# Counting edges: the second one-hot laid out with its steps innermost, and read by TensorE with a stride

## The chip, the cores and the metric

The kernel runs on one core of one Trainium2 chip. The metric is the device time of the whole program in microseconds (us), the median of three runs; lower is better.

## The reference

The reference is a stack of four graph layers (a GraphConv with batch norm, a SAGE layer pair, an attention layer and two relational layers) on 3125 nodes with 128 features and 103125 directed edges. All four take the same edge list, sorted by destination. The first two need, for every node, the sum of its neighbours' feature rows:

```
edge_index = jnp.stack([src, dst])
h = jnp.maximum(_layernorm(x, axis=-1), 0.0)
aggr = jax.ops.segment_sum(h[src], dst, num_segments=x.shape[0])      # layer 0
h = aggr @ W_rel + b_rel + x @ W_root                                 # then batch norm, relu, + x
agg = jax.ops.segment_sum(h[edge_src], edge_dst, num_segments=N) * inv_deg   # layer 1, twice
```

## The kernel before

The kernel does those sums as dense products with a matrix of edge counts, adj, which it builds first and keeps in DRAM. This stage, the edge counting, is the one that the change touches; it runs from about 62 us to 484 us of the profiled execution. Everything after it (the dense products of L794, the attention rounds, the relational layers with their gathers) is the same in both kernels.

**What is counted.** The edges lie in 806 tiles of 128, sorted by destination. A step is one tile of edges against one block of four destination nodes. There are 1596 steps, in 84 epochs of 19 (`EPOCHS`, `STEPS_OF`). For one step, an edge with source node s and destination d becomes two one-hot rows: one of 128 for the low seven bits of s (`hot_lo`), and one of 100 (`CELLS`) for its cell, which joins the high bits of s (25 values) with the place of d in the block (4 values) (`hot_cell`). TensorE multiplies the two, with the 128 edges as the contraction: the result, 128 x 100, holds the edge counts of this step, and adds up in PSUM at the place of its block.

**The three engines of an epoch.** VectorE makes the one-hots of an epoch in two instructions (`compare_epochs`): L677 compares `iota_lo` (the numbers 0 to 127, each written 19 times in a row) with the epoch's low bits, and L679 compares `iota_cell` (the numbers 1 to 100, once) with the epoch's cell numbers. There are two buffers of each one-hot; the comparison of epoch e waits until the matmuls of epoch e - 2 are done (`estep_n`). TensorE (`count_edges`) loads the epoch's 20 places from `steprow` into registers (L694), clears four PSUM banks with matmuls of zeros (L702, which waits for the eviction of epoch e - 2), waits for the one-hots of the epoch (`ehot_n`), issues 19 matmuls with one register operation ahead of each for the place (L706), then adds the overlap with the epoch before from SBUF (L711, which waits for the eviction of epoch e - 1), and closes the four banks (L715). ScalarE (`move_out`) evicts the half of PSUM into a window in SBUF (L737). Four epochs fill one window, and SP stores it to adj in DRAM (L759, 3850 KB). Between epochs 16 and 41 VectorE also takes the moments of one tile of x per epoch (L487).

**The layouts.** The low one-hot has the step innermost: its columns for one step lie 19 elements of 2 bytes, that is 38 bytes, apart. TensorE loads it as the weights of the step. The cell one-hot has the cell innermost, so the 100 columns of one step lie side by side. TensorE reads it as the moving operand.

**Before the stage.** `iota_ci` (int32, 1 to 100) is copied to `iota_cell` in L293 on ScalarE, and `iota_lo` written in L294. L362 writes `los`, L404 writes `cells`. `bs` (`step_block`) holds the block of every step, 1596 numbers, until L402.

Of the kernel before, what the change touches and what calls it, by code (L numbers as in the profile page):

```python
# [7 lines left out]
F16 = mybir.dt.float16  # L8
B16 = mybir.dt.bfloat16
ALU = mybir.AluOpType  # L10
ACT = mybir.ActivationFunctionType
# [3 lines left out]
P = 128  # L15
# [30 lines left out]
CELLS = HI * WD  # L46
KT = 7
STEPS_OF = 19
# [3 lines left out]
STEPS = EPOCHS * STEPS_OF  # L52
# [59 lines left out]
def build(nc, a, out):  # L112
    with ExitStack() as ctx:
# [6 lines left out]
        V = Lane(nc.vector, sem("s_dve"))  # L120
        A = Lane(nc.scalar, sem("s_act"))
# [20 lines left out]
        B1T = trio[:, NP:2 * NP]  # L142
# [62 lines left out]
        dense = ExitStack()  # L205

        def tmp(stack, name, shape, dt=F32):
            return stack.enter_context(nc.sbuf_tensor(name, shape, dt))
# [3 lines left out]
        los = tmp(dense, "edge_lo", [P, EPOCHS, STEPS_OF], F16)  # L212
        cells = tmp(dense, "edge_cell", [P, EPOCHS, STEPS_OF], F16)
        iota_lo = tmp(dense, "iota_lo", [P, P, STEPS_OF], F16)
        iota_cell = tmp(dense, "iota_cell", [P, CELLS], F16)
        steprow = tmp(dense, "steprow", [1, EPOCHS, 32], I32)
        dstf = invdeg[:, 4 * P:(4 + KT) * P].rearrange("p (k e) -> p k e", e=P)
        relf = invdeg[:, (4 + KT) * P:(4 + 2 * KT) * P].bitcast(F16)[:, 0:KT * P].rearrange("p (k e) -> p k e", e=P)
# [4 lines left out]
        early = ExitStack()  # L223
# [12 lines left out]
        iota_ci = tmp(early, "iota_ci", [P, CELLS], I32)  # L236
# [1 line left out]
        pid = tmp(early, "pid", [P, KT])  # L238
        first_d = tmp(early, "block_first", [P, KT])
        starts = tmp(early, "block_starts", [P, KT])  # L240
        bs = tmp(early, "step_block", [P, STEPS])
        rels = iota_si[:, :].bitcast(F32)
        inside = lower[:, 0:2 * STEPS].bitcast(F32)
        b0 = tmp(early, "epoch_block", [1, EPOCHS])
# [40 lines left out]
        cio = G.did(G.after().iota(iota_ci[:, :], pattern=[[1, CELLS]], base=1, channel_multiplier=0))  # L285
# [4 lines left out]
        G.did(G.after().iota(pieceidx[:, :], pattern=[[P, PT]], base=0, channel_multiplier=1))  # L290
        ios = A.did(A.after(sio).activation(iota_s[:, :], iota_si[:, :], ACT.Copy))
        iof = A.did(A.after(io).activation(iota[:, :], iota_i[:, :], ACT.Copy))
        A.did(A.after(cio).activation(iota_cell[:, :], iota_ci[:, :], ACT.Copy))  # L293
        A.did(A.after().activation(iota_lo[:, :, :], iota[:, :].unsqueeze(2).to_broadcast([P, P, STEPS_OF]), ACT.Copy))  # L294

        V.did(V.after(pio).tensor_copy(pid[:, :], pid_i[:, :]))
# [3 lines left out]
        for g in range(KT):  # L300
            m = V.did(nc.vector.tensor_scalar(lower[:, g * ET:(g + 1) * ET], dlast[:, :], first_d[:, g:g + 1], 0.0,
                                              ALU.is_lt, ALU.add, accum_out=starts[:, g:g + 1]))
# [3 lines left out]
        for g in range(KT):  # L306
            m = V.did(nc.vector.tensor_scalar(past[:, g, :], iota_s[:, :], starts[:, g:g + 1], None, ALU.is_ge))
# [22 lines left out]
        for k in range(KT):  # L330
            m = V.did(nc.vector.tensor_scalar(at_tile[:, k, :], ts[:, :], pid[:, k:k + 1], None, ALU.is_equal))
# [22 lines left out]
        for b, terms in ((4, (0,)), (0, (1,))):  # L354
            for j in range(4):
                for k in range(KT):
                    m = nc.tensor.matmul(pb[b + j][:, 0:QUARTER], digits[:, terms[0], k, :],
                                         at_tile[:, k, j * QUARTER:(j + 1) * QUARTER],
                                         start=(k == 0), stop=(k == KT - 1))
            looked = T.did(m)  # L360
            if b == 4:
                lod = A.did(A.after(looked).activation(los[:, :, :].rearrange("p e k -> p (e k)")  # L362
                                                       .rearrange("p (j c) -> p j c", c=QUARTER),
                                                       bank[:, 4:8, 0:QUARTER], ACT.Copy))
        T.need(lod)
        for j in range(4):
            for k in range(KT):
                for q in (2, 3):
                    m = nc.tensor.matmul(pb[4 + j][:, 0:QUARTER], digits[:, q, k, :],
                                         at_tile[:, k, j * QUARTER:(j + 1) * QUARTER],  # L370
                                         start=(k == 0 and q == 2), stop=(k == KT - 1 and q == 3))
# [272 lines left out]
        def turn_bank(j, src, folded, add):  # L644
            T.need(folded[j])
            tiles = tiles_of_bank(j)
            for i, t in enumerate(tiles):
# [6 lines left out]
        filled = [tmp(build, "adj_window", [P, SPANNED * CELLS]), arena[:, 0:SPANNED * CELLS]]  # L654
        LO, CELL = P * STEPS_OF // 2, STEPS_OF * CELLS // 2
        hot_lo = [t[:, 0:LO].bitcast(F16).rearrange("p (l k) -> p l k", k=STEPS_OF) for t in (B1T, HT)]
        hot_cell = [B1T[:, LO + j * CELL:LO + (j + 1) * CELL].bitcast(F16).rearrange("p (k c) -> p k c", c=CELLS)
                    for j in (0, 1)]
        G.need(V.now(), T.now(), A.now())
        wiped = [G.did(nc.gpsimd.memset(filled[j][:, SLOTS * CELLS * (1 - j):], 0.0)) for j in (0, 1)]  # L660
# [5 lines left out]
        first_norm = {}  # L666

        def compare_epochs():
            V.after()
            for e in range(EPOCHS):  # L670
                if e == 1:
                    V.need(s_seg.now())
                if e == MOMENTS_FROM:
                    V.need(s_x.now())
                if e > 1:
                    nc.vector.wait_ge(estep_n, e - 1)
                nc.vector.tensor_tensor(hot_lo[e % 2][:, :, :], iota_lo[:, :, :],  # L677
                                        los[:, e, :].unsqueeze(1).to_broadcast([P, P, STEPS_OF]), ALU.is_equal)
                nc.vector.tensor_tensor(hot_cell[e % 2][:, :, :],  # L679
                                        iota_cell[:, :].unsqueeze(1).to_broadcast([P, STEPS_OF, CELLS]),  # L680
                                        cells[:, e, :].unsqueeze(2).to_broadcast([P, STEPS_OF, CELLS]),
                                        ALU.is_equal).then_inc(ehot_n, 1)
                if MOMENTS_FROM <= e < MOMENTS_FROM + NT:
                    tile_moments(X, [e - MOMENTS_FROM])
                if e == VARIANCE_AT:
                    first_norm["variance"] = rows_variance(0, NT)
                if e == SHIFT_AT:
                    first_norm["shift"] = rows_shift(0, NT, (root_n, 1))

        def count_edges():  # L690
            T.need(stepped, A.now())
            for e in range(EPOCHS):
                half = sums[:, (e % 2) * 2048:(e % 2 + 1) * 2048]
                place = nc.values_load_multi_w_load_instructions(  # L694
                    steprow[0:1, e, 0:SLOTS], engines=(ENG.PE,), min_val=0, max_val=(SPANNED - 1) * CELLS,
                    skip_runtime_bounds_check_because="made on the chip from counts")[1]
                place = [nc.s_assert_within(v, 0, 2048 - CELLS, skip_runtime_bounds_check_because="made on the chip")
                         for v in place[:STEPS_OF]] + [place[STEPS_OF]]
                if e > 1:
                    nc.tensor.wait_ge(eout_n, e - 1)  # L700
                for j in range(4):
                    nc.tensor.matmul(half[:, j * 512:j * 512 + SLOTS // 4 * CELLS], zeros[:, 0:P],  # L702
                                     zeros[:, 0:SLOTS // 4 * CELLS], start=True, stop=False)
                nc.tensor.wait_ge(ehot_n, e + 1)
                for k in range(STEPS_OF):
                    m = nc.tensor.matmul(half[:, bass.ds(place[k], CELLS)], hot_lo[e % 2][:, :, k], hot_cell[e % 2][:, k, :],  # L706
                                         start=False, stop=False)
                m.then_inc(estep_n, 1)
                if e:
                    nc.tensor.wait_ge(eout_n, e)  # L710
                    nc.tensor.matmul(half[:, 0:CELLS], ident[:, :],  # L711
                                     filled[(e - 1) // GROUP % 2][:, bass.ds(place[STEPS_OF], CELLS)],
                                     start=False, stop=False)
                for j in range(4):
                    m = nc.tensor.matmul(half[:, j * 512:j * 512 + 1], zeros[:, 0:P], zeros[:, 0:1], start=False, stop=True)  # L715
                m.then_inc(ebuilt_n, 1)
# [60 lines left out]
        dense = ExitStack()  # L777
# [123 lines left out]
        for c in range(NCH):  # L901
# [4 lines left out]
            m = T.did(nc.tensor.matmul(pb[b][:, 0:CH], Wt["L0_root"][:, :], HT[:, s], start=False, stop=True))  # L906
# [7 lines left out]
        m = V.did(V.after().tensor_scalar(var, var, EPS, None, ALU.add))  # L914
        m = A.did(A.after(m).activation(bn["sd"][:, :], var, ACT.Sqrt))
# [4 lines left out]
        m = V.did(V.after().tensor_tensor(bn["shift"][:, :], bn["shift"][:, :], bcol["L0_beta"][:, :], ALU.add))  # L920
# [3 lines left out]
        for b, tiles in groups():  # L924
            m = A.did(nc.scalar.activation(cols_of(HT, tiles), cols_of(B1T, tiles), ACT.Relu, bias=bn["shift"][:, 0:1],
                                           scale=bn["scale"][:, 0:1]))
            T.need(m, last_evac[b])
            for j, t in enumerate(tiles):
                m = T.did(nc.tensor.transpose(pb[b][:, j * P:(j + 1) * P], HT[:, t * P:(t + 1) * P], ident[:, :]))
# [43 lines left out]
        for g in range(0, NT + 4, 4):  # L973
            tiles = list(range(g, min(g + 4, NT)))
            if tiles:
                b, m = products(tiles, "L1_n0", "L1_s0")
# [91 lines left out]
        m = V.did(V.after().tensor_scalar(pairnode[:, :], pairnode[:, :], 1.0, None, ALU.add))  # L1068
# [361 lines left out]
        for g in range(0, PAIRS, 4):  # L1430
# [3 lines left out]
            for j in js:  # L1434
                m = nc.tensor.transpose(pb[b][:, (j - g) * P:(j - g + 1) * P], pairs[:, j * P:(j + 1) * P], ident[:, :])
            m = T.did(m)
# [15 lines left out]
        m = V.now()  # L1452
# [230 lines left out]
```

## Time and profile before

| | |
|---|---|
| median of three runs | 4267.49 us (4274.33, 4267.49, 4263.15) |
| span of the profiled execution | 4266.3 us |
| time of the profiled execution beside the span | none given; its span lies 1.2 us under the median |
| TensorE matmul busy in the span | 3043.3 us (71%) |
| VectorE busy | 2017.8 us (47%) |
| GpSimd busy | 2364.9 us (55%) |
| edge counting, first to last DVE compare | 62.4 to 475.6 us |

The span is the time from the first instruction to the last on the core. PE is TensorE's matmuls, PEld its weight loads, PEldq and PEq its sequencer; DVE is VectorE, ACT ScalarE, POOL GpSimd, SP SyncE. A busy share over the whole span mixes stages; the prediction reads the edge counting alone. "issue" is idle time for which the profile shows no releaser. PEclk is the granted clock of TensorE, 1.00 for 2.4 GHz and 0.50 for 1.2 GHz.

### The profile page before, as it was taken

How to read it: one execution, taken by the hardware profiler on the slowest of the kernel's cores; microseconds unless marked ns; L12 is line 12 of the kernel's file. 1: busy time of each engine (PE TensorE's matmuls, PEld its weight loads, DVE VectorE, ACT ScalarE, POOL GpSimd, SP SyncE). 2: the span in 40 equal slices, each digit the busy share in tenths (PEclk: the TensorE clock that was granted, in tenths of full speed). 3: DMA queues.
4: the chain of work that ended last, by engine and by line, in shares of the span. 5: the costliest groups of instructions: out<-in, count | busy, mean ns of one | idle time of the engine just before them, and what ended most of it. 6: DMA issues, size and time to landing. Idle time of an engine off the chain costs nothing.

```text
span 4266.3 us, 42581 instructions
## 1 busy us (share of the span) xinstructions
PE 3043.3 (71%) x12281; PEld 2000.6 (47%) x12281; DVE 2017.8 (47%) x4124; ACT 705.0 (17%) x1923; POOL 2364.9 (55%) x2466
## 2 busy tenths in 40 slices
PE   5666798996888888888376666666667666666666
PEld 3555454554666666565243333333344333433334
DVE  7777685467988888898631111111112111111112
ACT  2334201002444444343320000000001000000000
POOL 3000000004777777776237777777775777777776
PEclk8778898998999999899675555555557555555555
DMA  3544754463444444443041111111123111111112
GB/s 125 214 191 194 302 215 190 200 263 97 119 115 114 118 110 118 110 118 97 3 149 53 53 53 53 53 53 52 53 70 142 53 53 53 52 53 53 52 53 63
DMA packets 236740, 456.14 MB, mean 107 GB/s; under 512 B 64036, under 2 KB 183570, under 8 KB 231392
## 3 DMA queue, kind: packets, MB, share of 16 engines
q1 hardware_dynamic: 158728, 291.44, 18.8%
q0 software_dynamic: 77792, 161.98, 13.9%
q8 instruction: 113, 1.85, 0.2%
q14 instruction: 107, 0.88, 0.1%
HBM read 336.68 MB, written 116.51 MB: 106 GB/s over the span
## 4 chain that ended last, share of the span: by engine, by line
POOL 37%; PE 26%; issue 17%; DMA 15%; DVE 4%; ACT 2%; SPq 0%; ACTq 0%; DVEq 0%; POOLq 0%
POOL edge_buffers L574 21%; POOL round_buffers L1124 16%; DMA edge_buffers<-rel_table,relidx 13%; PE sums L794 9%; PE sums L602 4%; PE sums L706 3%; PE sums L702 3%; PE sums L1582 2%; PE sums L711 1%; ACT adj_window L737 0%; DMA adj<-adj_window 0%; ACT chunk_and_window L737 0%; DMA adj_chunk<-adj 0%; PE sums L1246 0%; DVE tile_moments L487 0%
## 5 line engine op out<-in xcount | busy, mean ns | idle before, releaser
L574 POOL DMA_INDIRECT edge_buffers<-rel_table,relidx x1612 | 1534.2, 952 | 586.0 <-PE sums L602 268.8
L602 PE MATMUL sums<-edge_buffers 128*128 128x128 f32 x3224 | 1254.7, 495 | 750.2 <-DMA edge_buffers<-rel_table,relidx 746.4
L602 PEld LDWEIGHTS sums<-edge_buffers 128*128 128x128 f32 x3224 | 802.1, 310 | 1206.0 <-issue 1205.1
L585 DVE TENSOR_SCALAR edge_buffers<-iota,rel 128x128 f32<-128x128 f32 x1612 | 335.2, 296 | 1644.4 <-PE sums L602 1644.4
L1124 POOL DMA_INDIRECT round_buffers<-xs_t,srcs x806 | 765.5, 950 | 570.9 <-DMA xd_t<-round_buffers 325.5
L631 ACT ACTIVATE trio<-sums,c_L_b 128x256 f32<-128x256 f32 (+1 forms) x16 | 8.0, 500 | 2020.4 <-PE sums L606 2020.4
L944 POOL IOTA trio<- 128x806 int32 x1 | 0.8, 805 | 603.8 <-ACT H L517 603.8
L1168 PE MATMUL sums<-round_buffers,ident 128*128 128x408 f32 x620 | 278.6, 533 | 27.6 <-DMA round_buffers<-xs_t,srcs 24.1
L1171 PEld LDWEIGHTS sums<-round_buffers 128*128 128x128 f32 x1612 | 243.5, 198 | 76.1 <-issue 65.6
L1268 ACT ACTIVATE trio<-sums 128x128 f32 x806 | 223.7, 278 | 279.7 <-PE sums L1246 196.7
L1171 PE MATMUL sums<-round_buffers 128*128 128x136 f32 x1612 | 244.8, 285 | 0.0
L1246 PE MATMUL sums<-round_buffers 128*128 128x128 f32 x1612 | 241.7, 300 | 3.7 <-DVE round_buffers L1329 2.0
L794 PE MATMUL sums<-chunk_and_window,H 128*128 128x448 f32 x600 | 232.4, 548 | 7.7 <-issue 6.4
L1246 PEld LDWEIGHTS sums<-round_buffers 128*128 128x128 f32 x1612 | 217.3, 210 | 17.4 <-issue 14.5
L702 PE MATMUL sums<-zeros 128*128 128x500 f16 x336 | 110.4, 463 | 134.8 <-issue 131.7
L1320 DVE TENSOR_TENSOR positive<-positive,sums 128x384 f32<-128x384 f32 x310 | 153.1, 494 | 71.7 <-ACT positive L1258 71.4
L679 DVE TENSOR_TENSOR trio<-iota_cell,edge_cell 128x1900 f16<-128x1900 f16 x84 | 179.0, 2130 | 0.0
L677 DVE TENSOR_TENSOR trio<-iota_lo,edge_lo 128x2432 f16<-128x2432 f16 x84 | 125.2, 1491 | 112.4 <-PE sums L706 110.0
L794 PE MATMUL sums<-adj_chunk,H 128*128 128x448 f32 x450 | 172.4, 543 | 2.3 <-DMA adj_chunk<-adj 2.3
L794 PEld LDWEIGHTS sums<-chunk_and_window,H 128*128 128x128 f32 x600 | 115.5, 194 | 120.4 <-issue 118.6
L1309 DVE TENSOR_SCALAR round_buffers<-sums,pair_column 128x416 f32<-128x416 f32 x248 | 159.9, 645 | 11.5 <-PE sums L1186 10.3
L706 PEld LDWEIGHTS sums<-trio 128*128 128x128 f16 x1596 | 149.2, 151 | 28.7 <-issue 17.6
(289 smaller groups left out, 3000.0 us busy)
## 6 DMA issues: line engine op xcount, KB each, us to landing
chunk_and_window<-adj SPq DMA_DIRECT2D x10, 5600.0 KB, 15.8
round_buffers<-xd_t SPq DMA_DIRECT2D x806, 68.0 KB
adj_chunk<-adj SPq DMA_DIRECT2D x9, 5600.0 KB, 16.5
adj<-adj_window SPq DMA_DIRECT2D x11, 3850.0 KB, 11.5
adj<-chunk_and_window SPq DMA_DIRECT2D x10, 3850.0 KB, 11.3
edge_buffers<-rel_table,relidx POOLq DMA_INDIRECT x1612, 2.5
rel_table<-table_stages SPq DMA_DIRECT2D x50, 512.0 KB, 2.6
round_buffers<-xs_t,srcs POOLq DMA_INDIRECT x806, 2.5
```

The lines of the kernel that those rows point to most:

```text
L574: nc.gpsimd.indirect_dma_start(slot(t), None, table[:, :], bass.IndirectOffsetOnAxis(ap=index[:, t:t + 1], axis=0)).then_inc(slot_sem(t), 16)
L585: made = nc.vector.tensor_scalar(round_hots(i)[:, k, :], iota[:, :], rel[:, t:t + 1], None, ALU.is_equal)
L602: nc.tensor.matmul(sums[:, bass.ds(place[k], P)], slot(t), round_hots(i)[:, k, :], start=False, stop=False).then_inc(summed_n, 1)
L679: nc.vector.tensor_tensor(hot_cell[e % 2][:, :, :], iota_cell[:, :].unsqueeze(1).to_broadcast([P, STEPS_OF, CELLS]), cells[:, e, :].unsque ...
L702: nc.tensor.matmul(half[:, j * 512:j * 512 + SLOTS // 4 * CELLS], zeros[:, 0:P], zeros[:, 0:SLOTS // 4 * CELLS], start=True, stop=False)
L706: m = nc.tensor.matmul(half[:, bass.ds(place[k], CELLS)], hot_lo[e % 2][:, :, k], hot_cell[e % 2][:, k, :], start=False, stop=False)
L794: m = nc.tensor.matmul(ps.rearrange("p (b w) -> p b w", w=WD), tables[:, hi, :], held[b][:, :, hi, :], start=(hi == 0), stop=(hi == HI - 1))
L1124: nc.gpsimd.indirect_dma_start(rows[r % RING][:, k * RW:(k + 1) * RW], None, xs_t[:, :], bass.IndirectOffsetOnAxis(ap=srcs[:, t:t + 1], ax ...
L1168: nc.tensor.matmul(pb[2 + q % 2][:, 0:(hi - lo) * RW], ident[:, :], rows[r % RING][:, lo * RW:hi * RW], start=True, stop=False)
L1171: m = nc.tensor.matmul(pb[2 + q % 2][:, (k - lo) * RW:(k - lo + 1) * RW], hotT[r % 2][:, k * P:(k + 1) * P], win[r % 2][:, k * RW:(k + 1) ...
L1246: m = nc.tensor.matmul(pb[6 + q % 2][:, (k - lo) * P:(k - lo + 1) * P], msg[:, k * P:(k + 1) * P], hot[r % 2][:, k * P:(k + 1) * P], start ...
L1268: nc.scalar.activation(pairs[:, bass.ds(at[k], P)], pb[6 + q % 2][:, (k - lo) * P:(k - lo + 1) * P], ACT.Copy).then_inc(out_n, 1)
```

## The change

The numbers 1 to 100 are now written 19 times each (`iota_cell` is 128 x 100 x 19), the cell one-hot has the step innermost as the low one has, and L679 becomes an instruction whose three operands all run along 19 neighbouring elements. TensorE's moving operand `hot_cell[e % 2][:, :, k]` then has its 100 elements 38 bytes apart. To write the larger table ScalarE loses the copy of 100 elements ahead of `iota_lo` and gets one of 1900 elements behind L362; VectorE waits for it once, ahead of the first epoch. `bs` moves into a free part of `B1T`, which makes room in SBUF; nothing else changes its place.

```
-        iota_cell = tmp(dense, "iota_cell", [P, CELLS], F16)
+        iota_cell = tmp(dense, "iota_cell", [P, CELLS, STEPS_OF], F16)
-        bs = tmp(early, "step_block", [P, STEPS])
+        bs = B1T[:, 0:STEPS]
-        A.did(A.after(cio).activation(iota_cell[:, :], iota_ci[:, :], ACT.Copy))
+        A.need(cio)
                                                        bank[:, 4:8, 0:QUARTER], ACT.Copy))
+        cells_numbered = A.did(nc.scalar.activation(iota_cell[:, :, :],
+                                                    iota_ci[:, :].unsqueeze(2).to_broadcast([P, CELLS, STEPS_OF]), ACT.Copy))
-        hot_cell = [B1T[:, LO + j * CELL:LO + (j + 1) * CELL].bitcast(F16).rearrange("p (k c) -> p k c", c=CELLS)
+        hot_cell = [B1T[:, LO + j * CELL:LO + (j + 1) * CELL].bitcast(F16).rearrange("p (c k) -> p c k", k=STEPS_OF)
-            V.after()
+            V.after(cells_numbered)
-                nc.vector.tensor_tensor(hot_cell[e % 2][:, :, :],
-                                        iota_cell[:, :].unsqueeze(1).to_broadcast([P, STEPS_OF, CELLS]),
-                                        cells[:, e, :].unsqueeze(2).to_broadcast([P, STEPS_OF, CELLS]),
+                nc.vector.tensor_tensor(hot_cell[e % 2][:, :, :], iota_cell[:, :, :],
+                                        cells[:, e, :].unsqueeze(1).to_broadcast([P, CELLS, STEPS_OF]),
                                         ALU.is_equal).then_inc(ehot_n, 1)
-                    m = nc.tensor.matmul(half[:, bass.ds(place[k], CELLS)], hot_lo[e % 2][:, :, k], hot_cell[e % 2][:, k, :],
+                    m = nc.tensor.matmul(half[:, bass.ds(place[k], CELLS)], hot_lo[e % 2][:, :, k], hot_cell[e % 2][:, :, k],
```

On ScalarE's queue the start of the program reads, before:

```order
 L291 ACTIVATE iota_s<-chunk_and_window 128x1596
 L292 ACTIVATE iota<-iota_i 128x128
-L293 ACTIVATE iota_cell<-iota_ci 128x100
 L294 ACTIVATE iota_lo<-iota 128x2432
 L320 ACTIVATE digits<-hi_i 128x896
 L321 ACTIVATE digits<-hi_i 128x896
 L362 ACTIVATE edge_lo<-sums 128x1596
```

The row marked with a minus is gone from there in the changed kernel. The same queue of the changed kernel, from the evacuation of the low bits (`edge_lo`) to the transposed weights (`w_L_...`) and the loads of the stage, with its own line numbers:

```order
6 L362 ACTIVATE edge_lo<-sums 128x1596
7 L365 ACTIVATE iota_cell<-iota_ci 128x1900
8 L414 ACTIVATE w_L_s<-sums 128x128
9 L414 ACTIVATE w_L_n<-sums 128x128
10 L414 ACTIVATE w_L_s<-sums 128x128
11 L414 ACTIVATE w_L_n<-sums 128x128
12 L722 TENSOR_LOAD epochrow
```

The copy stands between L362 and the weights, where nothing stood before, and has grown from 100 to 1900 elements. On VectorE and TensorE no instruction changes its place.

## Rows read from the trace of the kernel before

**Rows 1.** The page, group 5: busy, mean ns of one, idle before and releaser

```profile
L679 DVE TENSOR_TENSOR trio<-iota_cell,edge_cell 128x1900 f16<-128x1900 f16 x84 | 179.0, 2130 | 0.0
L677 DVE TENSOR_TENSOR trio<-iota_lo,edge_lo 128x2432 f16<-128x2432 f16 x84 | 125.2, 1491 | 112.4 <-PE sums L706 110.0
```

**Rows 2.** The timeline of TensorE's matmuls, one window of four epochs

```profile
223.86 1.46 PE L702 MATMUL sums<-zeros 128*128 128x500 f16 x4 [0.90 <-issue]
230.76 1.53 PE L702 MATMUL sums<-zeros 128*128 128x500 f16 x4 [3.27 <-issue]
232.09 1.79 PE L706 MATMUL sums<-trio 128*128 128x100 f16 x19
233.68 0.71 PE L711 MATMUL sums<-adj_window,ident 128*128 x2
234.19 0.29 PE L715 MATMUL sums<-zeros 128*128 128x1 f16 x4
235.82 1.00 PE L702 MATMUL sums<-zeros 128*128 128x500 f16 x4 [1.35 <-issue]
236.66 1.85 PE L706 MATMUL sums<-trio 128*128 128x100 f16 x19
239.81 1.00 PE L702 MATMUL sums<-zeros 128*128 128x500 f16 x4 [0.90 <-issue]
240.65 1.91 PE L706 MATMUL sums<-trio 128*128 128x100 f16 x19
242.43 0.46 PE L711 MATMUL sums<-adj_window,ident 128*128 x2
242.73 0.24 PE L715 MATMUL sums<-zeros 128*128 128x1 f16 x4
243.87 1.00 PE L702 MATMUL sums<-zeros 128*128 128x500 f16 x4 [0.90 <-issue]
```

**Rows 3.** The line of the places' load: duration ns min/median/max, first and last start

```profile
L694 PEldq TENSOR_LOAD <-steprow x84: 1356/1383/4776, 64.5 to 477.5; - x84
```

**Rows 4.** The line of the 19 matmuls, 235.8 to 238.35 us only

```profile
L706 PEldq FUSED_REGOPS  x19: 37/37/42, 235.8 to 238.2; - x19
L706 PEld LDWEIGHTS sums<-trio x19: 136/138/159, 236.5 to 238.3; 128*128 128x128 f16 x19
```

**Rows 5.** The same line, 232.0 to 233.65 us (a stretch at half clock)

```profile
L706 PE MATMUL sums<-trio x19: 286/286/289, 232.1 to 233.6; 128*128 128x100 f16 x19
```

**Rows 6.** The line of the clearing matmuls, 235.7 to 236.4 us

```profile
L702 PEld LDWEIGHTS sums<-zeros x4: 96/96/96, 235.8 to 236.2; 128*128 128x128 f16 x4
```

**Rows 7.** The timeline of VectorE in the same window

```profile
226.94 1.49 DVE L677 TENSOR_TENSOR trio<-iota_lo,edge_lo 128x2432 f16<-128x2432 f16 x1 [0.60 <-PE sums L706]
228.35 2.13 DVE L679 TENSOR_TENSOR trio<-iota_cell,edge_cell 128x1900 f16<-128x1900 f16 x1
230.39 0.29 DVE L487 BATCH_NORM_STATS2 tile_moments<-X 128x6 f32<-128x128 f32 x1
235.33 2.13 DVE L679 TENSOR_TENSOR trio<-iota_cell,edge_cell 128x1900 f16<-128x1900 f16 x1
```

**Rows 8.** The timeline of SP's queue, 220 to 250 us

```profile
225.07 0.33 SPq L759 DMA_DIRECT2D adj<-chunk_and_window  x1
```

**Rows 9.** The timeline of ScalarE: the start, and one eviction

```profile
4.44 0.29 ACT L293 ACTIVATE iota_cell<-iota_ci 128x100 f16<-128x100 int32 x1
4.76 2.23 ACT L294 ACTIVATE iota_lo<-iota 128x2432 f16<-128x2432 f32 x1
18.89 0.95 ACT L320 ACTIVATE digits<-hi_i 128x896 bf16<-128x896 int32 x1 [11.90 <-DVE hi_i L319]
63.62 0.28 ACT L412 ACTIVATE w_L_s<-sums 128x128 f32<-128x128 f32 x1 [22.44 <-PE sums L409]
234.59 1.84 ACT L737 ACTIVATE adj_window<-sums 128x2000 f32 x1 [5.10 <-PE sums L715]
```

**Rows 10.** The chain that ended last, in the dense products: start, us, what

```profile
541.43 18.79 PE sums L794 x50
```

**Rows 11.** The page, group 6: DMA issues, KB each, us to landing

```profile
adj<-adj_window SPq DMA_DIRECT2D x11, 3850.0 KB, 11.5
```

## The prediction

> **What bounds the kernel now.** The change touches the edge counting alone, so I read that stage and not the shares of the whole span. First the page's groups: per epoch VectorE spends 1.491 us on the low one-hot and 2.130 us on the cell one-hot, and the only wait in front of them is 110 us in all on TensorE's matmuls of L706 [rows 1]. So VectorE waits for TensorE in this stage. Then TensorE's timeline over one window of four epochs [rows 2]: L702 starts at 223.86, 230.76, 235.82, 239.81 and 243.87, which makes epochs of 6.90, 5.06, 3.99 and 4.06 us, 20.01 us a window; 21 windows are 420 us. Ahead of each L702 TensorE is idle for 0.90 to 3.27 us with no releaser named. The line of the places' load names it: this register load takes 1.36 us at least and 4.78 us at most [rows 3]. The long ones fall right behind the store of a window, which SP issues at 225.07 [rows 8] and which lands 11.5 us later [rows 11]: I take them for loads that queue behind that store. Last, the pace inside an epoch: TensorE's sequencer issues the 19 register operations of L706 from 235.8 to 238.2, 2.4 / 18 = 0.13 us apart (with the first one's wait for the clearing matmuls; in the middle 0.12) [rows 4]. An epoch of the short kind is therefore 1.36 us of load and some 2.65 us of issue, 4.0 us: the **sequencer of TensorE** bounds it, not the array and not VectorE.
>
> How far VectorE is from the path: the one-hots of the comparison at 226.94 are done at 228.35 + 2.13 = 230.48, and the matmuls that read them start at 236.66 [rows 2, 7]; those done at 235.33 + 2.13 = 237.46 are read at 240.65. That is 6.2 and 3.2 us of slack.
>
> **VectorE's part.** L677 shows what the new form costs: 2432 elements in rows of 19 in 1491 ns. L679 with 1900 elements in the same form takes, in proportion, 1165 ns, and with a fixed part of some 150 ns set aside 1200 ns. I take 1200: 930 ns less per epoch, 84 x 0.93 = 78 us less busy time. None of it is on the path, since the slack above is larger than 0.93 us already; VectorE will wait longer for L706 instead. Its gain is 0. If the form did not speed up at all (bound from above), the result would be the same 0.
>
> **ScalarE's part.** The removed copy took 0.29 us, and 11.90 us of idle time stand behind L294 before L320 [rows 9]: 0. The new copy of 1900 elements lies between the 2.23 us of L294's 2432 elements and nothing, so about 1.8 us. It starts when L362 ends, near 41 us, and ScalarE is idle for 22.44 us until 63.62 [rows 9]; the first comparison comes at 62.4. TensorE's queue waits for L362 by its own mark, not for the new copy. 0, and if the cover were gone at most 1.8 us, once. Moving `bs` costs nothing: the same instructions on another address.
>
> **TensorE's part, the term that decides.** Each of the 1596 matmuls now reads its 100 moving columns 38 bytes apart. No matmul of the trace reads a moving operand so, therefore bounds. Contiguous, at half clock the 19 matmuls start from 232.1 to 233.6, 1.5 / 18 = 83 ns apart, which is 100 columns at 1.2 GHz [rows 5]; at full clock this is 42 ns. Free reading is the lower bound (nothing added). From above: L794 reads its moving operand in 112 runs of four elements of 4 bytes, 400 bytes apart, and takes 18.79 / 50 = 376 ns [rows 10], so a jump costs 3.36 ns at most; 100 jumps are 336 ns. Between them stands the nearest row, the weights of L706, which have this very stride: their load takes 138 ns, the contiguous weights of L702 take 96 ns [rows 4, 6]. The stride costs 42 ns on 128 columns. Spread over all 128 that is 0.33 ns a column, and a matmul would take 42 + 33 = 75 ns. If the load brings its columns in four at a time, 32 one behind the other, it is 1.3 ns a column, and a matmul takes 42 + 131 = 173 ns. I take the second, **170 ns**: a weight load that delivered one column at a time at the moving operand's full rate would already take 128 columns x 0.42 = 53 ns of its 96, and the rows of L715, four loads and matmuls in 0.24 us with their latency [rows 2], leave no room for 53 ns each.
>
> The page "Advanced Engine Details and Errata" of the Trainium skill, section SBUF Cachelines, says that SBUF has lines of 16 bytes, and that a reader needs two hits on a line to hide the memory's latency. A stride of 38 bytes hits each line once, so the rule speaks against this change; no run here shows its size for a moving operand. Read as "half the rate" it would give 83 ns a matmul at full clock, which the sequencer's 120 ns hide.
>
> From 170 ns the epoch follows. At full clock the array needs 0.84 us from L702's start to L706's (239.81 to 240.65), 19 x 0.17 = 3.23, then 0.30 for L711 and 0.10 for L715 (242.43 to 242.73, and four short ones) [rows 2]: 4.47 us. At half clock L702 takes about 1.5 and L711 with L715 0.6: 5.3 us. The load of the places runs beside the array's backlog, so an epoch takes the larger of sequencer and array:
> - 42 epochs of the short kind: 4.47 in place of 4.03, 42 x 0.44 = 18.5 us.
> - 21 second epochs at 5.06: hidden at full clock, 0.24 at half clock; taken as half of them, 3 us.
> - 21 first epochs of 6.90: the array is hidden, but matmuls that end later make the eviction later (1.84 us, [rows 9]), L711 waits for it, and the load queued behind L711 starts later: about 0.25, 5 us.
>
> Sum 26.5 us, all on the path, against a span of 4266.3: 4293 us. Added to the median, 1.2 us higher, **4294 us**. Behind the wait of L711 stand on TensorE's queue only L715 and the next load, counted above.
>
> **Rivals.**
> - A. No change. The strided read takes up to 115 ns a matmul (the 75 ns reading above, or half rate), and the sequencer's pace covers it: 4267 us. For it: 3.2 us of slack, and 45 to 78 ns of cover per matmul. Against: the array would have to read this stride at a seventh to a third of the jump price that L794 allows, which no row shows.
> - B. Much slower. Weights and moving operand now both jump through SBUF in the same instants and hinder each other: 240 ns a matmul, an array epoch of 0.84 + 4.56 + 0.40 = 5.8 us, so 42 x 1.77 + 21 x 0.9 + some 5 = 98 us: 4366 us. At the bound of 336 ns every epoch is array-bound at 7.6 us, 21 x (30.5 - 20.0) = 220 us: 4487 us. Nothing in the trace rules it out.
> - C. Faster. The long loads of the places are slowed not by the store alone but also by VectorE's traffic, of which 0.93 us per epoch goes. The loads beyond 1.36 us cost (6.90 - 4.0) + (5.06 - 4.0) = 4.0 us a window, 84 us in all; it needs a matmul of at most 115 ns, and if a quarter of the excess were the comparison's it gives 21 us: 4246 us. Against: the comparisons run in all four epochs, the excess stands only in the two behind the store. It decides from a tenth of the excess on.
>
> That L679 keeps its 2.13 us is part of A where the read is free: same time.
>
> **Chances.** The forecast, a matmul of 120 to 200 ns, 0.45; A 0.37; B 0.13; C 0.05. This kernel's measurement tells about 0.3% (13 us) from no change. Of the forecast's cases about 0.04 add less than 13 us (140 ns or below). So faster 0.05, same 0.40, slower 0.55. The likeliest case's own range is 4277 to 4325; the range that should hold eight in ten must take in A and the near half of B: 4262 to 4370.
>
> **What will show it.** In the profile of the changed kernel: L681 (the cell comparison) at about 1200 ns; a longer wait of L679 for the matmuls, by some 80 us and more; the new copy under 2 us near 41 us with idle time behind it. The step that decides is the spacing of the matmuls of L707 in a full-clock epoch: 0.17 us and an epoch of 4.5 us prove the forecast, 0.12 and 4.0 prove A, 0.24 and 5.8 prove B. The load of the places should still take 1.36 us at least; shorter long ones would speak for C. The prediction is wrong if the stage from the first comparison to the last eviction does not grow by 13 to 60 us, or if the time moves elsewhere.

## The result: slower by 1.9%, three times the forecast loss

The changed kernel takes 4348.91 us (median) against 4265.33 us before in the same session: ratio 1.0192, 95% interval 1.0175 to 1.0208, 84 us more by the medians. The forecast was 4294 us, 27 us more. One of the changed kernel's four executions took 11346.93 us, far from the others and unexplained; the ratio leaves it out, and the median of the other three is 4343.97 us. The direction and the strided read as its source came as forecast. The size did not, although 4348.91 us lies inside the stated range.

The page of the changed kernel begins so (span, then the same groups as in [rows 1]; L679 and L681 are the two comparisons there, L707 the 19 matmuls, L703 the clears):

```profile
span 4352.5 us, 42582 instructions
L707 PE MATMUL sums<-trio 128*128 128x100 f16 x1596 | 306.9, 362 | 0.0
L679 DVE TENSOR_TENSOR trio<-iota_lo,edge_lo 128x2432 f16<-128x2432 f16 x84 | 125.4, 1493 | 271.5 <-PE sums L707 268.2
L703 PE MATMUL sums<-zeros 128*128 128x500 f16 x336 | 149.2, 597 | 33.4 <-issue 31.7
```

Its line for the cell comparison, with duration min/median/max:

```profile
L681 DVE TENSOR_TENSOR trio<-iota_cell,edge_cell x84: 1190/1194/1200, 63.9 to 557.9; 128x1900 f16<-128x1900 f16 x84
```

VectorE got what it was to get, 1194 ns in place of 2130. It waits 268.2 us for the matmuls where it waited 110.0 [rows 1]. TensorE's timeline of one window, which answers to [rows 2]:

```profile
275.94 1.83 PE L703 MATMUL sums<-zeros 128*128 128x500 f16 x4
277.56 3.65 PE L707 MATMUL sums<-trio 128*128 128x100 f16 x19
281.03 0.60 PE L712 MATMUL sums<-adj_window,ident 128*128 x2
281.42 0.29 PE L716 MATMUL sums<-zeros 128*128 128x1 f16 x4
281.58 1.83 PE L703 MATMUL sums<-zeros 128*128 128x500 f16 x4
283.20 3.67 PE L707 MATMUL sums<-trio 128*128 128x100 f16 x19
286.68 0.59 PE L712 MATMUL sums<-adj_window,ident 128*128 x2
288.55 1.82 PE L703 MATMUL sums<-zeros 128*128 128x500 f16 x4 [1.19 <-issue]
294.46 1.82 PE L703 MATMUL sums<-zeros 128*128 128x500 f16 x4
```

Two things have changed. From L707's start to L712's, 19 matmuls, it is 286.68 - 283.20 = 3.48 us: **183 ns a matmul**. And most of the 0.90 to 3.27 us waits ahead of the clears are gone. TensorE is idle for 33.4 us in all ahead of L703; ahead of the same clears before it was 134.8 us:

```profile
L702 PE MATMUL sums<-zeros 128*128 128x500 f16 x336 | 110.4, 463 | 134.8 <-issue 131.7
```

The epochs of 5.64 us (275.94 to 281.58) hold no idle time, so the array bounds them. The clears start some 0.42 us apart at half clock, and 1.62 us go from L703's start to L707's, where the full-clock epoch of before had 0.84.

The stage as a whole, by the view of stretches, of before and of the changed kernel (busy of PE, PEld, DVE, ACT, POOL; then the granted clock):

```profile
68.14:484.20 416.06, 283.57 (x2434) 221.71 (x2432) 298.71 (x199) 165.37 (x111) 7.71 (x2) 0.81 0.47 198
```

```profile
68.14:570.30 502.16, 471.20 (x2434) 319.83 (x2434) 222.46 (x199) 165.44 (x111) 7.82 (x2) 0.56 0.40 168
```

The stage is 86.1 us longer and the span 86.2 us: all of the loss is here. What follows takes 4266.3 - 484.2 = 3782.1 us before and 4352.5 - 570.3 = 3782.2 us after. The granted clock of the stage fell from 0.81 to 0.56: 67 of the 83 distances between epochs run at half clock throughout, where it was 14 before. Where the clock is full, the changed kernel's epoch is shorter with the same matmuls:

```profile
162.11 1.00 PE L703 MATMUL sums<-zeros 128*128 128x500 f16 x4
162.95 3.63 PE L707 MATMUL sums<-trio 128*128 128x100 f16 x19
166.40 0.56 PE L712 MATMUL sums<-chunk_and_window,ident 128*128 x2
166.91 1.41 PE L703 MATMUL sums<-zeros 128*128 128x500 f16 x3
```

This epoch takes 166.91 - 162.11 = 4.80 us, with 182 ns a matmul. **The 19 strided matmuls take the same time at either clock; the clears and L712 do not**, and they make the 0.84 us by which the epoch of 5.64 us is longer. (The clock is full up to L712 here, which takes 0.56 us as at half clock.)

### The profile page after: what moved, and what is told of

Read it like the earlier page. It is cut to its first block, busy times and chain, and to the rows that moved or that the text cites. A ratio compares the mean times of both kernels' runs of the same rounds, so it can differ in the third digit from the quotient of the medians.

```text
span 4352.5 us, 42582 instructions
## 1 busy us (share of the span) xinstructions
PE 3225.0 (74%) x12281; PEld 2094.8 (48%) x12281; DVE 1940.1 (45%) x4124; ACT 706.3 (16%) x1923; POOL 2369.7 (54%) x2466
## 4 chain that ended last, share of the span: by engine, by line
PE 34%; DMA 24%; POOL 24%; issue 12%; DVE 5%; ACT 1%; SPq 1%; DVEq 0%; ACTq 0%; POOLq 0%
DMA edge_buffers<-rel_table,relidx 22%; POOL round_buffers L1125 13%; POOL edge_buffers L576 10%; PE sums L795 9%; PE sums L604 7%; PE sums L707 7%; PE sums L703 3%; PE sums L1583 2%; PE sums L1169 1%; PE sums L712 1%; PE sums L1247 1%; PE sums L1172 1%; DVE logits L1324 1%; DVE positive L1321 0%; DMA adj_chunk<-adj 0%
## 5 line engine op out<-in xcount | busy, mean ns | idle before, releaser
L707 PE MATMUL sums<-trio 128*128 128x100 f16 x1596 | 306.9, 362 | 0.0
L707 PEld LDWEIGHTS sums<-trio 128*128 128x128 f16 x1596 | 227.2, 142 | 101.5 <-issue 41.1
L679 DVE TENSOR_TENSOR trio<-iota_lo,edge_lo 128x2432 f16<-128x2432 f16 x84 | 125.4, 1493 | 271.5 <-PE sums L707 268.2
L703 PE MATMUL sums<-zeros 128*128 128x500 f16 x336 | 149.2, 597 | 33.4 <-issue 31.7
```

## The experiments

Stage means from the first comparison to the end of the last eviction: 421.8 us before, 507.8 us in the changed kernel. Runs e5 to e10 were taken on two other chips, on which the whole program is some 850 us longer, the kernel before too (5120 us). In e5's trace the extra time lies behind the edge counting (4629 us against 3782). The kernel before left no trace on those chips, so their stages are set beside the 421.8 us from the first one; that this may be done is borne out by e5, whose stage and the changed kernel's agree to 0.1 us. Differences of whole programs are of the medians.

### e1: the read alone, first try

```
-        hot_cell = [... .rearrange("p (k c) -> p k c", c=CELLS)
+        hot_cell = [... .rearrange("p (c k) -> p k c", k=STEPS_OF)
```

> Only the read is changed: VectorE makes the cell one-hot with the operands of before (100 cells innermost, the cell number repeated), but writes it with the step innermost, so that TensorE's moving columns lie 38 bytes apart as in the changed kernel. Output as the reference's. Theory (TensorE's strided read costs 183 ns a matmul and the clock stays at half): all of the loss is here, 4340 to 4360 us, the matmuls 183 ns apart, epochs of 5.6 us, although the comparison keeps about 2.1 us. Rival (the new comparison or the new copy takes part in the loss, for instance by disturbing TensorE's reads of SBUF): clearly under 4340 us, spacing under 183 ns.

Measured: 4649.26 us, ratio 1.0908 (1.0891 to 1.0924). This was a bad experiment. VectorE now writes each element 38 bytes from the last, and that is what the run shows:

```profile
L679 DVE TENSOR_TENSOR trio<-iota_cell,edge_cell x84: 8381/8408/8437, 62.7 to 864.6; 128x1900 f16<-128x1900 f16 x84
```

8.41 us in place of 2.13 makes VectorE the bound (no idle time before either comparison). It says nothing on the size of the loss, except that the matmuls stand 183 ns apart here too, with a quite different VectorE beside them.

### e5: the read alone, with VectorE as before

```
+        step_of = [f.rearrange("p (c k) -> p c k", k=STEPS_OF) for f in flat_cell]
-  ... hot_cell[e % 2][:, k, :],
+  ... step_of[e % 2][:, :, k],
```

> The read alone, with VectorE exactly as before (both comparisons write as before, 1.49 and 2.13 us); TensorE takes its 100 moving columns 38 bytes apart from the same buffer, so the edge counts are not those of the reference. Theory (the loss is TensorE's strided read and nothing else): 4344 to 4354 us, spacing 183 ns, epochs of 5.6 us, the clock at half nearly throughout. Rival (the new comparison helps or hurts beside it): off by more than 10 us from the changed kernel.

Measured: ratio 1.0181 (1.0156 to 1.0205), 84 us more than before; the stage 507.7 us against the changed kernel's 507.8. The cell comparison kept its 2.13 us. The timeline has the same epoch:

```profile
276.07 1.83 PE L703 MATMUL sums<-zeros 128*128 128x500 f16 x4
277.69 3.65 PE L707 MATMUL sums<-trio 128*128 128x100 f16 x19
281.16 0.60 PE L712 MATMUL sums<-adj_window,ident 128*128 x2
281.70 1.83 PE L703 MATMUL sums<-zeros 128*128 128x500 f16 x4
```

The read makes the whole loss. With 3.62 us of comparisons or 2.69, an epoch takes 5.63 to 5.64 us. The read also brings the clock down: it is the only change against the kernel before, and the granted clock of the stage is 0.55 where it was 0.81.

### e2: the comparison alone

```
-  ... hot_lo[e % 2][:, :, k], hot_cell[e % 2][:, :, k],
+  ... hot_lo[e % 2][:, :, k], flat_cell[e % 2][:, k * CELLS:(k + 1) * CELLS],
```

> Only the comparison is changed: the one-hots are made as in the changed kernel (comparison of 1.19 us), but TensorE reads 100 neighbouring elements as the moving operand, so the edge counts are not those of the reference. Theory (VectorE is off the path): 4262 to 4270 us, no change from before, VectorE waits for the matmuls some 80 us more. Rival (VectorE's time counts in the short epochs, or its traffic lengthens the loads of the places): 4240 to 4255 us, short epochs under 4.0 us or the long loads under 4.3 us.

Measured: 4263.48 us against 4264.02, ratio 1.0002 (0.9993 to 1.0011); stage 421.7 us. Nearly all of the 78 us that VectorE saves becomes wait, 185.2 us for the matmuls in place of 110.0:

```profile
DVE trio L679 <- PE sums L707: 185.2, 82, 5.3
```

So rival C is out, which needed a gain of 8 us or more: neither VectorE's time nor its traffic was in the loads of the places, of which 20 still take 4.3 us or more, as before.

### e3: half of the columns

```
+  half[:, bass.ds(place[k], CELLS // 2)], hot_lo[e % 2][:, :, k], hot_cell[e % 2][:, 0:CELLS // 2, k],
```

> The changed kernel, but every matmul of the counting reads only the first 50 of its 100 strided columns (the other half of the counts is left out). Theory (a price of 1.83 ns per column read, whatever the clock): 92 ns a matmul at most, which the sequencer's 120 ns hide, so the loss is gone: 4262 to 4272 us. Rival (a fixed price for a matmul with a strided operand): spacing stays over 150 ns and the time over 4310 us.

Measured: 4267.88 us, ratio 1.0011 (1.0002 to 1.0021), the matmuls 95 to 96 ns apart. Half of the columns cost half of the time, so the price goes by the column. This run also separates the clock from the loss; its stage:

```profile
68.14:484.00 415.86, 342.65 (x2408) 251.49 (x2407) 221.97 (x199) 162.85 (x110) 7.22 (x2) 0.50 0.46 194
```

The granted clock was half throughout, and the whole stage took 426.9 us, 5 us more than before. Here, where the array has room to spare, half clock costs at most these 5 us; in the changed kernel, where the array bounds the epochs, it costs 0.84 us an epoch.

### e4: a table of strides in one run

Each window of four epochs reads its operands in another way:

```
+  READS = ((1, 19, 100), (2, 19, 100), ..., (19, 1, 100), (1, 1, 100), ..., (19, 19, 50), (19, 19, 25))
+  return (flat_lo[e % 2][:, k:k + ws * (P - 1) + 1:ws], flat_cell[e % 2][:, ko:ko + s * (n - 1) + 1:s], n)
```

> A table in one run: the 21 windows of four epochs read the operands of the counting matmuls with 21 combinations of the moving stride (1 to 19 elements of 2 bytes), the weights' stride (19, 4 or 1) and the number of columns (100, 75, 50, 25); the edge counts are not those of the reference. Theory (a moving column costs 1.83 ns once each lies on a line of its own, less below, and the weights have no part): about 183 ns at strides of 8 elements and more, falling below that, the same with contiguous weights, 137 ns with 75 columns, the sequencer's 120 ns or the backlog's 60 ns with 50 and 25. Rival (weights and moving operand hinder each other): with contiguous weights at moving stride 19 the spacing falls clearly, towards 100 ns.

Measured in one execution (4308.72 us): from the starts of the matmuls in the trace, the median distance in the window's epochs in ns (s: moving stride in elements of 2 bytes, w: stride of the weights, n: columns). Strides 1 and 2 are given where the array has a backlog at full clock; elsewhere the sequencer or the clock sets their distance.

```
w 19, n 100:  s 1: about 60   s 2: 63   s 3: 77   s 4: 97   s 5: 119   s 6: 140   s 7: 162   s 8: 184
              s 9: 188   s 10: 186   s 12: 182   s 16: 186   s 18: 184   s 19: 183
other:        s 19 w 1: 180   s 8 w 1: 179   s 4 w 4: 94   s 19 n 75: 139   s 19 n 50: 95   s 19 n 25: 60
```

Four rows of its timeline at stride 5, then four at stride 8, then two with contiguous weights (L714 are the clears, L719 the matmuls, L724 what follows):

```profile
143.73 2.43 PE L719 MATMUL sums<-trio 128*128 128x100 f16 x19
145.98 0.38 PE L724 MATMUL sums<-chunk_and_window,ident 128*128 x2
151.45 2.45 PE L719 MATMUL sums<-trio 128*128 128x100 f16 x19
153.72 0.66 PE L724 MATMUL sums<-adj_window,ident 128*128 x2
...
225.25 1.83 PE L714 MATMUL sums<-zeros 128*128 128x500 f16 x4
226.87 3.68 PE L719 MATMUL sums<-trio 128*128 128x100 f16 x19
230.37 0.60 PE L724 MATMUL sums<-chunk_and_window,ident 128*128 x2
230.91 1.83 PE L714 MATMUL sums<-zeros 128*128 128x500 f16 x4
...
395.49 3.61 PE L719 MATMUL sums<-trio 128*128 128x100 f16 x19
398.92 0.59 PE L724 MATMUL sums<-adj_window,ident 128*128 x2
```

(145.98 - 143.73) / 19 = 118 ns, (230.37 - 226.87) / 19 = 184 ns, (398.92 - 395.49) / 19 = 181 ns. From stride 3 to 8 the distance grows by 20 to 22 ns per element of stride, and then it stays between 180 and 188 ns. A stride of 8 elements is 16 bytes. So the price is about **1.84 ns for each piece of 16 bytes that the read newly touches**: at stride 8 and above each column touches one, at stride 4 two columns share one (50 x 1.84 = 92, measured 97). This is a fit to the table, good to 2 ns from stride 6 to 8 and 4 to 8 ns too low from 3 to 5. Contiguous weights take off 3 to 5 ns: the two operands hardly hinder each other, and rival B's mechanism is out.

The page "Advanced Engine Details and Errata" of the Trainium skill, section SBUF Cachelines, has the 16 bytes right, by this table. Its "at least two hits on a cacheline" is not enough for this 2-byte moving operand: stride 4 has two hits and takes 97 ns, where stride 1 shows about 60 and single distances down to 44 ns.

### e6: does more dense work bring the clock back?

```
-                for j in range(4):
+                for j in range(8):      # the second four add zeros
```

> The changed kernel, with the four clearing matmuls of each epoch issued twice (the second four add zeros). It adds 0.84 us of dense array work per epoch at full clock, 1.67 us at half. Theory (the half clock comes from the strided reads, which leave the array waiting for its operand, and 19 x 0.183 us of them per epoch keep it down whatever stands beside them): epochs of 5.63 + 1.67 = 7.3 us, some 4455 us. Rival (more dense work brings the full clock back): 4.80 + 0.84 = 5.6 us an epoch, 4350 us, and the granted clock of the stage well over 0.56.

Measured: 5286.92 us, ratio to before 1.0337; stage 584.8 us, 77 us over the changed kernel's. The view of stretches:

```profile
100.00:480.00 380.00, 357.71 (x1822) 227.64 (x1821) 149.58 (x143) 104.57 (x62) 0.00 (x0) 0.76 0.34 144
```

Neither expectation holds alone. The granted clock rose from 0.56 to 0.76, with nothing but the four added clears an epoch: so the strided matmuls do not hold the clock at half whatever stands beside them. But every window still has epochs at half clock in part or throughout, and the time lies between the two forecasts. Some epochs run at full clock from end to end:

```profile
250.65 1.85 PE L703 MATMUL sums<-zeros 128*128 128x500 f16 x8
252.33 3.63 PE L707 MATMUL sums<-trio 128*128 128x100 f16 x19
256.11 1.85 PE L703 MATMUL sums<-zeros 128*128 128x500 f16 x8
```

This one takes 256.11 - 250.65 = 5.46 us; without the second four clears (0.84 us) it would be 4.62 us, an estimate of the changed kernel's epoch at full clock. That the strided read brings the clock down is shown by e5, and that dense work beside it brings part of it back by e6; what it is in the strided matmuls that does it stays open.

### e7: a layout that TensorE reads cheaply

```
+ iota_cell = tmp(dense, "iota_cell", [P, CELLS, 4], F16)
+ hot_cell = [t[:, LO:LO + SLOTS * CELLS // 2].bitcast(F16).rearrange("p (g c k) -> p g c k", k=4, c=CELLS) for t in (B1T, HT)]
+ ... hot_cell[e % 2][:, k // 4, :, k % 4],
```

> The cell one-hot in groups of four steps, the step of the group innermost: VectorE's operands run along 4 neighbouring elements, TensorE's moving columns lie 8 bytes apart; the output is the reference's. Theory (a matmul costs 1.84 ns for each line of 16 bytes that it newly reads, two columns to a line here): about 97 ns, under the sequencer's 120 ns, 4260 to 4270 us, no change from before, with the comparison at 1.2 to 1.3 us. Rival (short rows cost VectorE its gain, or a spacing of 97 ns at half clock still delays the evictions): over 4275 us.

Measured: ratio 1.0018 (1.0002 to 1.0035); stage 422.6 us, before's 421.8. The comparison takes 1.46 us, not 1.2 to 1.3, and the matmuls stand 97 ns apart:

```profile
240.03 1.00 PE L706 MATMUL sums<-zeros 128*128 128x500 f16 x4 [0.85 <-issue]
240.87 1.98 PE L710 MATMUL sums<-trio 128*128 128x100 f16 x19
242.72 0.46 PE L715 MATMUL sums<-adj_window,ident 128*128 x2
244.16 1.00 PE L706 MATMUL sums<-zeros 128*128 128x500 f16 x4 [0.90 <-issue]
```

An epoch takes 244.16 - 240.03 = 4.13 us with 0.90 us of idle time, as in [rows 2]. The loss is gone and VectorE keeps 0.67 us per epoch, which nothing needs. The granted clock is 0.81 over the stage as before, although the matmuls stand as far apart as in e3, where it was 0.50: the distance alone does not decide the clock.

### e8 to e10: is it the sequencer that paces the kernel before?

e8 is the kernel before with three loads of places a window (20, 32 and 28 numbers) in place of four of 20:

```
+                if e % GROUP == 1 and e > 1:
+                    place = ahead
+                elif e % GROUP == 0 and e:
+                    got = load_places(e * SLOTS + 12, 28)
+                    place, ahead = [*ahead, *got[:8]], got[8:]
+                elif e % GROUP == 3 and e < EPOCHS - 1:
+                    got = load_places(e * SLOTS, 32)
+                    place, ahead = got[:SLOTS], got[SLOTS:]
```

> The kernel before, with the places of a window loaded by three register loads in place of four, and none in the epoch right behind the store's start (20, 32 and 28 numbers, each used one epoch later at the latest); comparisons, matmuls and layouts as before. Theory (the sequencer of TensorE with these loads paces the epochs): a window loses 1.4 us at least and 3.3 us where the slow load goes with it, 21 x 1.4 to 3.3 = 29 to 69 us, so 4195 to 4236 us, limited by VectorE's 3.6 to 3.9 us per epoch. Rival (the array, VectorE or the eviction sets the pace, and the loads are slow because something else is late): within 10 us of before.

Measured: stage 406.2 us against 421.8, 15.6 us less; the whole program 5110.59 against 5119.94 us, ratio 0.9985 (0.9971 to 1.0000), an interval that reaches no change. This is less than the 29 to 69 us expected. The line of the loads (duration ns min/median/max), and the clears of two epochs in the timeline:

```profile
L693 PEldq TENSOR_LOAD <-steprow x64: 1360/2130/4910, 64.8 to 462.2; - x64
```

```profile
239.48 1.00 PE L716 MATMUL sums<-zeros 128*128 128x500 f16 x4 [0.85 <-issue]
242.27 1.00 PE L716 MATMUL sums<-zeros 128*128 128x500 f16 x4
```

The epoch without a load takes 242.27 - 239.48 = 2.8 us (median 2.98 in the 21 windows), where a short epoch with its load took 4.0, so the load was on the path. But 32 numbers take 2.13 us and 28 take 1.88 where 20 take 1.36, in proportion to their count; and the first load behind the start of the window's store still takes some 4.4 us, only one epoch later. Of what was saved, this leaves 0.75 us a window.

e9 puts e8's loads and e7's layout together.

> The three register loads a window of e8, with the one-hot in groups of four steps of e7; the output is the reference's. Theory (the loads and the issue of TensorE's sequencer pace the stage, VectorE stays off the path even in the shorter windows): the stage as in e8, 406 us, some 4249 us where the kernel before takes 4265. Rival (in e8 VectorE's 3.6 to 3.9 us held back the epoch without a load): clearly shorter than e8, 395 us and 4238 us or less.

Measured: 5105.00 against 5121.69 us, ratio 0.9974 (0.9960 to 0.9989); stage 408.8 us, e8's 406.2. VectorE's 0.67 us bring nothing even here. This is the only version whose interval lies below 1, by 0.1 to 0.4%; by the stage alone e8 is as good or 2.6 us better.

e10 puts e8's loads into the changed kernel.

> The changed kernel with the three register loads a window of e8. Theory (with the strided read the array bounds the epochs, 5.6 us, and the loads run beside it, except the slow one): only the place of the slow load moves, windows of 23.9 us in place of 24.1, 4340 to 4349 us. Rival (the sequencer still paces the changed kernel, its loads late because the queue is full): as large a gain as in e8 or larger, 4333 us or less.

Measured: ratio to before 1.0166 (1.0138 to 1.0193); stage 501.9 us, 5.9 us under the changed kernel's. The epoch without a load, 2.8 us in e8, takes 284.78 - 279.13 = 5.65 us here at half clock (median 5.43):

```profile
279.13 1.83 PE L717 MATMUL sums<-zeros 128*128 128x500 f16 x4
280.75 3.67 PE L721 MATMUL sums<-trio 128*128 128x100 f16 x19
```

So the sequencer paces the kernel before, and the array the changed one.

## Why the prediction was wrong

- **VectorE's gain of 930 ns an epoch is worth 0**: right. 936 ns were measured, and e2 made no difference (1.0002).
- **ScalarE's copy is hidden**: right. It took 1.78 us at 41.18 us, with 20.77 us of idle time behind it.
- **What bounds the stage before**: right. The sequencer with its loads, shown by e8 and e10. That the long loads queue behind the store is borne out by e8, where the load that now meets the store's start is the long one.
- **170 ns a matmul**: near, 183 ns, but partly by luck. The prediction drew 131 ns from the weights of the same stride and added them to the 42 ns of 100 columns at full clock. With the 83 ns of half clock the same sum gives 214 ns, and 183 were measured at half clock too. Nor do the weights pay the moving operand's price: 128 x 1.84 would be 236 ns, and their load takes 140. So "four columns at a time" is not shown; it only gave a number near the right one. Rival A (75 or 83 ns) and rival B (240 ns, for a reason that e4 excludes) were wrong. In rival B's sum 21 x 0.9 should be 21 x 0.74 by its own 5.8 and 5.06 us, 3 us less; nothing rests on it.
- **"At full clock the array needs ... 4.47 us. At half clock ... 5.3 us", and then 42 short epochs at 4.47**: this step failed. The prediction took the clock of before over into the changed kernel. With 183 ns the two figures are 4.80 and 5.64 us, both seen in the trace; but nearly all epochs ran at the second. By the kinds of the prediction and the median of each kind in the trace: short epochs 42 x (5.64 - 4.03) = 68 us, forecast 18.5; second epochs 21 x (5.90 - 5.06) = 18 us, forecast 3; first epochs 21 x (6.98 - 6.90) = 2 us, forecast 5. Together 87 us, against 86 measured. (In 5 of the 21 windows the first epoch takes 4.80 us at full clock and the second 7.3 in its place.) Of the 60 us that were missed, 13 ns x 19 = 0.25 us an epoch, some 10 to 15 us, are the size of the read; the rest, some 45 us, is the clock. With 4.62 us, the estimate of e6 for full clock, the short epochs would have lost 42 x (4.62 - 4.03) = 25 us and not 68.
- That the clock causes that part is read from the trace (the two kinds of epoch with the same 183 ns) and borne out by e5, where the read alone brought the clock down, by e3, where half clock under a read that the sequencer hides cost 5 us at most, and by e6, where the clock rose. No run has the strided read at full clock throughout, so the 45 us are worked out and not measured as a whole.

## What to carry to other kernels

Before you make an operand cheap to write, ask what its reader pays: here 1.84 ns for every 16 bytes newly touched turned matmuls of 42 to 83 ns into 183 ns. An operand of 2-byte elements can be written in groups of four steps, so that the stride is 8 bytes, and here both sides were content (97 ns a matmul, a comparison of 1.46 us). And where a change makes the array the bound, work out its epoch at half clock too: in this kernel the array stood idle less than before and was granted less, 0.56 in place of 0.81, and the four clears took 1.62 us in place of 0.84.

## What was not expected of the hardware

- The strided read costs the same at either clock, 182 ns at full and 183 ns at half.
- Matmuls 95 to 97 ns apart ran at a granted clock of 0.50 in e3 (50 columns, stride of 38 bytes) and of 0.81 in e7 (100 columns, stride of 8 bytes).
- A VectorE comparison that writes each 2-byte element 38 bytes from the last takes 8.41 us for 1900 elements, 4.4 ns each, against 1.1 ns written side by side (e1).
- A load of registers costs by the number: 1.36, 1.88 and 2.13 us for 20, 28 and 32 values, 0.064 us each; right behind the start of a window's 11 us store it takes 3.8 to 4.9 us.
